# Group statistics of a convolution kernel: column sums on TensorE, and two loads per pair of channels

## The reference, cut to what matters

```python
def _gn(v, G=16, eps=1e-5):
    g = v.reshape(B_, G, C_ // G, H_, W_)
    m = jnp.mean(g, axis=(2, 3, 4), keepdims=True)
    s = jnp.var(g, axis=(2, 3, 4), keepdims=True)
    return ((g - m) / jnp.sqrt(s + eps)).reshape(v.shape)

x = x + _L0_conv_ref(_gn(x), weight, bias)          # 3x3 convolution, input and weights rounded to int8 levels
x = x + _L1_conv_ref(_gn(x), R_real, R_imag)        # low-frequency mixing of channels by rfft2 and irfft2
```

## Time and profile before

| | us |
|---|---|
| median of 3 runs | 3830.03 |
| range of the runs | 3829.28 to 3840.93 |
| the profiled execution | 3835.66 |
| its span, first to last instruction | 3833.7 |

### The profile page before, as it was taken

The page is one execution under the profiler, slowest core; times in us unless marked ns, Lnnn a source line. Parts: engine busy times, 40 slices in busy tenths (PEclk is TensorE's granted clock), DMA queues, the critical chain, the costliest instruction groups (busy, mean ns, idle before and its releaser), DMA issues.

```text
span 3833.7 us, 79482 instructions
## 1 busy us (share of the span) xinstructions
PE 2790.1 (73%) x31386; PEld 1545.5 (40%) x31481; DVE 3377.8 (88%) x3462; ACT 2547.4 (66%) x3507; POOL 823.1 (21%) x1040
## 2 busy tenths in 40 slices
PE   0010000069999999999999999898888888888886
PEld 0000000036666666666666666673222222222222
DVE  6999999999999999999999999559888888888887
ACT  8999999958888787878788888433333333333332
POOL 0000000035445454545454545200000000000000
PEclk9999999999999999999999999859999999999998
DMA  9999999989999999999999999629999999999998
GB/s 361 357 357 357 356 354 357 344 223 354 344 306 348 304 356 297 354 301 351 311 342 326 332 336 315 207 96 422 427 427 427 427 427 427 427 423 420 420 419 372
DMA packets 323941, 1352.20 MB, mean 353 GB/s; under 512 B 43600, under 2 KB 44848, under 8 KB 241616
## 3 DMA queue, kind: packets, MB, share of 16 engines
q1 hardware_dynamic: 204528, 811.10, 58.8%
q0 software_dynamic: 82272, 268.58, 19.6%
q10 hardware_dynamic: 36864, 268.45, 16.6%
HBM read 811.09 MB, written 536.87 MB: 352 GB/s over the span
## 4 chain that ended last, share of the span: by engine, by line
DMA 37%; DVE 32%; PE 13%; issue 11%; ACT 5%; SPq 0%; POOL 0%; ACTq 0%; DVEq 0%
DMA out<-ring 20%; DVE ring L568 11%; DMA ring<-in_x 9%; DMA ring<-x_scratch 7%; DVE area L550 6%; PE ps L713 4%; DVE area L545 4%; DVE area L554 3%; ACT area L300 3%; PE ps L724 2%; DVE ring L663 2%; DVE area L563 2%; ACT area L308 2%; PE ps L816 1%; PE ps L734 1%
## 5 line engine op out<-in xcount | busy, mean ns | idle before, releaser
L284 POOL DMA_DIRECT2D x_scratch<-ring x1024 | 817.1, 805 | 1613.6 <-DVE ring L568 1590.8
L858 PE MATMUL ps<-x,gj_s 128*128 128x512 bf16 x2977 | 772.1, 408 | 218.5 <-DVE ring L663 211.6
L713 PE MATMUL ps<-area,wq 128*32 128x512 bf16 x12264 | 766.0, 383 | 57.8 <-DVE ring L568 32.2
L663 DVE TENSOR_TENSOR ring<-ps,ring 128x1024 f32<-128x1024 f32 x512 | 603.3, 1220 | 162.6 <-DMA ring<-x_scratch 159.2
L568 DVE SCALAR_TENSOR_TENSOR ring<-ps,sc,ring 128x1024 f32<-128x1024 f32 x512 | 634.3, 1279 | 20.0 <-PE ps L713 12.9
L339 ACT ACTIVATE area<-ps 128x512 f32<-128x512 f32 x1024 | 552.9, 595 | 115.8 <-PE ps L724 115.1
L469 DVE TENSOR_REDUCE stat<-area 128x4096 f32 (+1 forms) x128 | 565.5, 4418 | 55.9 <-ACT area L308 55.9
L858 PEld LDWEIGHTS ps<-x,gj_s 128*128 128x128 bf16 x3072 | 296.0, 103 | 772.6 <-DVE ring L663 437.0
L686 PE MATMUL ps<-stat,mean_s 128*128 x256 | 74.5, 360 | 693.9 <-DVE area L463 652.8
L724 PE MATMUL ps<-id_s,ring 128*128 128x128 f32 x4096 | 561.4, 280 | 17.5 <-ACT area L339 16.7
L346 ACT ACTIVATE area<-ring,qtab 128x2048 bf16<-128x2048 f32 x256 | 513.1, 2004 | 0.0
(11 more groups left out here) (122 smaller groups left out, 2349.7 us busy)
## 6 DMA issues: line engine op xcount, KB each, us to landing
ring<-in_x SPq DMA_DIRECT2D x128, 2048.0 KB, 8.5
ring<-in_x SPq DMA_DIRECT2D x1024, 256.0 KB, 6.9
x_scratch<-ring POOLq DMA_DIRECT2D x1024, 256.0 KB, 6.6
ring<-x_scratch SPq DMA_DIRECT2D x256, 1024.0 KB, 10.0
out<-ring ACTq DMA_DIRECT2D x256, 1024.0 KB, 27.0
ring<-in_rt SPq DMA_DIRECT2D x1, 4096.0 KB, 13.7
area<-in_gj SPq DMA_DIRECT2D x1, 768.0 KB, 4.5
eh_s<-in_eh SPq DMA_DIRECT2D x1, 128.0 KB, 2.1
```

Of the source, the lines that this page charges most:

```text
L284: pool.dma_start(x1_rows[b, m, r], xslot(t % SL)[32 * r:32 * r + 32, :].rearrange("p (g w) -> p g w", g=4)).then_inc(s_x_out[t % SL], 16)
L663: nc.vector.tensor_tensor(half, ps[0][:, hj * 2 * HW:(hj + 1) * 2 * HW], half, ALU.add).then_inc(s_add, 1)
L713: last = mm(ps[0][32 * cg:32 * cg + 32, HW * g:HW * g + HW], wq[:, (3 * a + dw) * C:(3 * a + dw + 1) * C], src[:, 1 + dw:1 + dw + HW], sta ...
L858: last = mm(bank(j), gj_s[:, (j * 3 + v) * 128:(j * 3 + v + 1) * 128], (z12, z12, z13)[v][:, k % 2], start=(v == 0), stop=(v == 2))
```

## The change

Three things change in the first stage.

1. The sum of a group is taken on TensorE. The weight is `negm_s`, 128x32, filled with -1/N. Eight fp32 matmuls per group, each over 512 of the 4096 columns, write into one PSUM bank: the column slices j and j + 4 accumulate on partitions 32(j % 4) to 32(j % 4) + 31. What is left, 128x512 in PSUM, is summed over its row by ScalarE (even groups) or VectorE (odd groups) into a column of a new tile `part`. The mean matmul then multiplies this column by a matrix with ones in rows 0, 32, 64 and 96. The banks of the column sums are 0 to 3, those of the means 4 to 7.
2. TensorE's order becomes: column sums of group n + 1, then the mean of group n. The column sums wait for the landing of their group (both transfers, semaphore at 32 per use).
3. The two channels of a group are loaded by two transfers, each 128 partitions x 2048 numbers (8 KB), one behind the other on SP's queue. The first channel now fills the first half of every partition of the slot, the second the other half.

The loops of the first stage are also written out in full where they were loops of the program with four groups in their body. There is one more constant to load.

```diff
@@ -39,7 +39,7 @@
     x1 = nc.dram_tensor("x1_scratch", [B, C, HW, HW], F32, kind="Internal").ap()
-    x_groups = x.rearrange("b (g c) (p h) w -> (b g) (c p) (h w)", c=GC, p=64)
+    x_chan = x.rearrange("b c (p j) w -> (b c) p (j w)", j=NJ)
@@ -69,6 +69,8 @@
         bsel_s = sb("bsel_s", [NT, B])
+        negm_s = sb("negm_s", [128, C])
+        part = sb("part", [128, NT])
@@ -94,8 +96,7 @@
             return ps[k // 4][0:p, (k % 4) * 512:(k % 4 + 1) * 512]
-        junk_v = area[:, 0:FT // 2]
-        junk_a = area[:, FT // 2:FT // 2 + FT]
+        junk_a = area[:, 0:HW]
@@ -149,6 +150,7 @@
         s_g_in = [sem(f"group_landed{k}") for k in range(4)]
+        s_cols = sem("group_column_sums_done")
@@ -206,7 +208,7 @@
         s_add = sem("out_done")
-        NCONST = 12
+        NCONST = 13
@@ -215,17 +217,15 @@
                              (gsel_s[:], gsel), (bsel_s[:], bsel), (comb_s[:], comb),
-                             (gsum_s[:], gsum), (gbc_s[:], gbc), (pavg_s[:], pavg)):
+                             (gsum_s[:], gsum), (gbc_s[:], gbc), (pavg_s[:], pavg), (negm_s[:], negm)):
                 sp.dma_start(dst, src).then_inc(s_const, 16)
-            for k in range(4):
-                sp.dma_start(gslot(k), x_groups[k]).then_inc(s_g_in[k], 16)
-            with sp.Fori(1, NT // 4) as i:
-                for k in range(4):
-                    sp.wait_ge(s_sq, i * 4 + (k - 3))
-                    sp.dma_start(gslot(k), x_groups[ds(i * 4 + k, 1)].rearrange("o p f -> (o p) f")).then_inc(
-                        s_g_in[k], 16)
+            for n in range(NT):
+                if n >= 4:
+                    sp.wait_ge(s_sq, n - 3)
+                for c in range(GC):
+                    sp.dma_start(gslot(n % 4)[:, c * FC:(c + 1) * FC], x_chan[GC * n + c]).then_inc(s_g_in[n % 4], 16)
@@ -295,30 +295,24 @@
         def _(act):
-            def group_sum(k, landed, n):
-                act.wait_ge(s_g_in[k], landed)
-                act.activation(junk_a, gslot(k), ACT.Identity, accum_out=st(0, n)).then_inc(s_asum, 1)
-            def squares(k, n, free):
+            def group_sum(n):
+                act.wait_ge(s_cols, n + 1)
+                act.activation(junk_a, bank(n % 4), ACT.Identity, accum_out=part[:, n:n + 1]).then_inc(s_asum, 1)
+            def squares(n):
                 act.wait_ge(s_mean, n + 1)
-                act.activation(st(1, n), bank(k)[:, 0:1], ACT.Copy).then_inc(s_nmean, 1)
+                act.activation(st(1, n), bank(4 + n % 4)[:, 0:1], ACT.Copy).then_inc(s_nmean, 1)
                 act.wait_ge(s_nmean, n + 1)
-                if free:
+                if n >= 2:
                     act.wait_ge(s_max, n - 1)
-                act.activation(sqs[:, k % 2], gslot(k), ACT.Square, bias=st(1, n),
+                act.activation(sqs[:, n % 2], gslot(n % 4), ACT.Square, bias=st(1, n),
                                accum_out=st(2, n)).then_inc(s_sq, 1)
-            for k in range(4):
-                if k % 2 == 0:
-                    group_sum(k, 16, k)
-                if k:
-                    squares(k - 1, k - 1, k - 1 >= 2)
-            with act.Fori(1, NT // 4) as i:
-                for k in range(4):
-                    if k % 2 == 0:
-                        group_sum(k, i * 16 + 16, i * 4 + k)
-                    squares((k - 1) % 4, i * 4 + (k - 1), True)
-            squares(3, NT - 1, True)
+            group_sum(0)
+            for n in range(NT):
+                if n % 2 and n + 1 < NT:
+                    group_sum(n + 1)
+                squares(n)
@@ -458,27 +452,20 @@
             link(nc.vector.memset(ones_s[:], 1.0))
-            def group_sum(k, landed, n):
-                dve.wait_ge(s_g_in[k], landed)
-                nc.vector.scalar_tensor_tensor(out=junk_v, in0=gslot(k)[:, 0:FT // 2], scalar=0.0,
-                                               in1=gslot(k)[:, FT // 2:FT], op0=ALU.add, op1=ALU.add,
-                                               accum_out=st(0, n)).then_inc(s_dsum, 1)
-            def largest(k, n):
+            def group_sum(n):
+                dve.wait_ge(s_cols, n + 1)
+                nc.vector.tensor_reduce(part[:, n:n + 1], bank(n % 4), AXX, ALU.add).then_inc(s_dsum, 1)
+            def largest(n):
                 dve.wait_ge(s_sq, n + 1)
-                nc.vector.tensor_reduce(st(3, n), sqs[:, k % 2], AXX, ALU.max).then_inc(s_max, 1)
-            for k in range(4):
-                if k % 2:
-                    group_sum(k, 16, k)
-                if k:
-                    largest(k - 1, k - 1)
-            with dve.Fori(1, NT // 4) as i:
-                for k in range(4):
-                    if k % 2:
-                        group_sum(k, i * 16 + 16, i * 4 + k)
-                    largest((k - 1) % 4, i * 4 + (k - 1))
-            largest(3, NT - 1)
+                nc.vector.tensor_reduce(st(3, n), sqs[:, n % 2], AXX, ALU.max).then_inc(s_max, 1)
+            for n in range(NT):
+                if n % 2 == 0:
+                    group_sum(n + 1)
+                if n:
+                    largest(n - 1)
+            largest(NT - 1)
@@ -679,11 +666,24 @@
             pe.wait_ge(s_const, 16 * NCONST)
-            with pe.Fori(0, NT // 4) as i:
-                for k in range(4):
-                    pe.wait_ge(s_dsum if k % 2 else s_asum, i * 2 + (k // 2 + 1))
-                    mm(bank(k)[:, 0:1], mean_s[:], st(0, i * 4 + k), start=True, stop=True).then_inc(s_mean, 1)
+            def column_sums(n):
+                pe.wait_ge(s_g_in[n % 4], (n // 4 + 1) * 32)
+                if n >= 4:
+                    pe.wait_ge(s_mean, n - 3)
+                for j in range(8):
+                    g = j % 4
+                    last = mm(bank(n % 4)[32 * g:32 * g + 32, :], negm_s[:], gslot(n % 4)[:, j * HW:(j + 1) * HW],
+                              start=(j < 4), stop=(j >= 4))
+                last.then_inc(s_cols, 1)
+            column_sums(0)
+            for n in range(NT):
+                if n + 1 < NT:
+                    column_sums(n + 1)
+                pe.wait_ge(s_dsum if n % 2 else s_asum, n // 2 + 1)
+                if n >= 4:
+                    pe.wait_ge(s_nmean, n - 3)
+                mm(bank(4 + n % 4)[:, 0:1], mean_s[:], part[:, n:n + 1], start=True, stop=True).then_inc(s_mean, 1)
@@ -918,7 +918,7 @@
     return {n: np.ascontiguousarray(v, dtype=np.float32) for n, v in dict(
-        eh=eh, ew=ew, gj=gj, ei=ei, ident=np.eye(128), mean=np.full((128, 128), -1.0 / (GC * HW * HW)), gsel=gsel, bsel=bsel, comb=comb, gsum=gsum, gbc=gbc, pavg=pavg).items()}
+        eh=eh, ew=ew, gj=gj, ei=ei, ident=np.eye(128), mean=np.repeat(np.arange(128)[:, None] % C == 0, 128, 1), negm=np.full((128, C), -1.0 / (GC * HW * HW)), gsel=gsel, bsel=bsel, comb=comb, gsum=gsum, gbc=gbc, pavg=pavg).items()}
```

More of the change, by code:

```diff
@@ L24, with build @@
 NK = 2 * NS
-def build(nc, x, wt, bias, rt, eh, ew, gj, ei, ident, mean, gsel, bsel, comb, gsum, gbc, pavg, out):
+def build(nc, x, wt, bias, rt, eh, ew, gj, ei, ident, mean, gsel, bsel, comb, gsum, gbc, pavg, negm, out):
     B = x.shape[0]
```

## The result

The changed kernel took 3829.71 us (median of 20 runs, 3823.92 to 3836.87), the kernel before 3836.04 in the same comparison: ratio 0.9987, 95% interval [0.9981, 0.9993]. It is faster by 0.13% by the ratio (the medians lie 6 us apart), which is no change by the measure of the prediction; 82 us less than 3830.03 were forecast, and the range of 3696 to 3806 didn't hold it.

A forecast was written before the change was run, and what follows sets the result against it. ScalarE was taken to bound the first stage, then a three-group loop: (column sums + 5.0 + landing 7.7) / 3, mixed clock, 5.25 us per group; stage end 694.9, 82.0 us earlier, hence 3748 us; range 3696 to 3806.

The forecast's parts named there:

- The bound now: First stage before the change: ScalarE sets the pace at 5.86 us per group, then VectorE at 5.6, transfers only third.
- The column sums: Added on TensorE: eight fp32 matmuls per group, four side by side, 1.9 us at the upper clock, 3.6 at the lower.
- Rival (d): TensorE: column sums don't overlap four deep, 7.4 us per group, 192 us later, 4022; chance 0.12.
- The loop: First stage's new bound: column sums, 5.0 us of further work and issue to landing, spread over three groups; 5.25 us per group.
- The landing D: Time from a load's issue to its landing, in the first stage's loop: taken as 7.7 us.
- Rival (b): First stage: landings at their present median of 8.4 us, 5.67 us per group, 29 us earlier, 3801; chance 0.15.
- The share of the levels: TensorE's clock in the first stage: a third of the groups at the upper level, giving 5.25 us per group.
- Rival (c): First-stage transfers already at a limit of 357 GB/s for reads, 5.87 us per group, 3826, no change; chance 0.08.
- The split: Two loads per group: lands no later, at worst 0.13 us per group; 427 against 435 GB/s, inside the 4.9 us.

The follow-up runs named there:

- e4: Changed kernel with the mean of a group ahead of the next group's column sums on TensorE, short sum just ahead of its squares or largest; 3722.43 us, ratio 0.9715.
- e5: Changed kernel with its own order and split loads, but six slots for groups instead of four; 3727.28 us, ratio 0.9719.
- e11: Changed kernel with one more wait on SP: a group's loads are issued only once the group before has landed; 4044.8 us (one run).
- e1: Changed kernel with one transfer of 16 KB per partition per group instead of two, column sums on TensorE kept; 3839.04 us, ratio 1.0017.
- e3: Changed kernel with one transfer per group that still writes two pieces of 8 KB per partition; 3838.46 us, ratio 1.0012.
- e9: Changed kernel with TensorE's first stage as a loop of four groups instead of written out, same order and waits; 3835.56 us, ratio 1.0004.
- e7: Changed kernel with column sums that read one partition of the slot instead of 128; 3820.19 us, ratio 0.9958.
- e8: Changed kernel with eight more fp32 matmuls of 128 columns, result unused, behind each mean on TensorE; 3799.8 us, ratio 0.9914.
- e6: e4 with one transfer of 16 KB per partition per group instead of two; 3711.59 us, ratio 0.9676.
- e10: e6 with six slots for groups instead of four; 3712.12 us, ratio 0.9681.
- e2: Kernel before with only its first stage's loads split into two transfers of 8 KB per partition; 3838.0 us, ratio 1.0012.

## Why the prediction was wrong

**The bound now, right.** ScalarE set the stage at 5.88 us per group. The change took ScalarE and VectorE off the path as costed: the short sums took 0.590 and 0.690 us (0.6 and 0.7 forecast).

**The column sums, right.** 1.92 and 3.64 us at the two levels (1.9 and 3.6 forecast), four matmuls side by side; the mean is 387.4 / 128 = 3.03. Rival (d) didn't happen.

**The loop, right.** Landing n+1 to issue n+4 took 7.84 us; 3.0 + 5.0 = 8.0 was forecast. e4 and e5, which open the loop in two ways, gained 110 and 108 us on the kernel before. That "the mean matmul of group n stands in TensorE's order behind the column sums of group n+1" is shown to be what closes it over three groups.

**The landing D, wrong: the term that failed.** The passage is "here a load would be issued when the one before is nearly through, so I take 7.7". D was 9.58. A third of 1.9 us is 0.63 per group, times 126 it is 79 us, and that is nearly the whole gain that was forecast. Rival (b), late landings, had the right mechanism and too low an end: it took 8.4, the median of the earlier trace rows. The events of the kernel before show that this median lies between two kinds of landing, of which there are 58 each in groups 8 to 123. SP issued in pairs, some 4 and 7.7 us apart in turn. The first load of a pair was issued 1.5 us before the landing ahead of it and took 7.70; the second was issued 3.7 us before it and took 9.20. The forecast took the first kind for all. In the changed kernel the issue was 3.8 us before the landing ahead on average, the 48 loads issued over 4 us before it took 10.3, and the 32 issued only 2 to 3 us before it still took 8.85. So loads that bunch are a part of it and not all.

What the 1.9 us are. Against the kernel before, the middle engine is no later (7.68 and 7.75), and the last of the 16 engines is 1.90 us behind it where it had been 0.70. A group has landed only when all 16 are through. Against landings on empty engines (e11) the 2.1 us more are 0.6 of the middle engine and 1.5 of the last one. The split (e1, e3), the instruction fetches (e9) and, for the most part, TensorE's reads (e7) are not the cause. e11 shows what removes the spread: engines that are empty at each issue. The kernel before points the same way, with 0.41 us for the first load of a pair and 0.99 for the second.

How the spread builds up is open. In e7 it grows from 0.90 to 2.3 us over four loads behind one that was issued within 2.2 us of the landing ahead; but the same count in the changed kernel shows no growth (2.28 for that first load, 1.62 four loads later) and none in e9. So it is shown that the spread is there while loads are queued and gone when the engines are emptied, and not what delays an engine. In the changed kernel 93 of 100 packets of 8 KB took 0.3 to 0.4 us and single ones up to 2, and e11 has 94 of 100 like this with a spread of 0.37; in e4 all but 2 of 1000 took 0.3 to 0.4, and the spread was 1.60. The share of slow packets doesn't go with the spread. And no run has the loop of three groups at a small spread, so that the 79 us would come back is worked out, not measured.

**The share of the levels.** The mean of 3.03 us is what a third at the upper level gives ((1.92 + 2 x 3.64) / 3 = 3.07). By group it was 35 at the upper level throughout, 46 at the lower and 47 on both, so the weight was right, though it was guessed for landings 5.25 us apart and not 5.82, which makes it luck in part. e8 shows the price of it: 30 us between 3.0 and 2.1 us of column sums.

**Rival (c).** Reads alone go on at 421 to 428 GB/s in e4, e6 and e10. The rule of the Trainium skill ("DMA: Bandwidth & Descriptors", "Bandwidth") that the HBM share of 358 GB/s binds would have given the right time for the wrong reason; that of "HBM Reference" ("Specifications (TRN2)"), that a core alone goes well above its share, agrees with these rows. That both kernels stood at 357 to 361 GB/s was chance, and so was the unchanged time: one bound, ScalarE's 5.88 us per group, was taken away, and the next one, the loop's 5.82, happened to lie 0.06 below it.

**The split.** Forecast inside the 4.9, and it cost 0.07 us per group where the transfers bind (e6). Where the loop binds it cost nothing: e1 and e3, with one transfer, were if anything slower than the changed kernel (1.0017 and 1.0012 against 0.9987). Why isn't shown.

**The range.** It ended at T = 5.67. The row for its upper end was there: D had a maximum of 10.9, and a queued load took 9.36. With 9.4 the prediction's own sum gives (8.05 + 9.4) / 3 = 5.82 and 3820; with 10.9 it gives 6.3, more than ScalarE's time before. I had ruled out queueing on the ground that a load would be issued when the one before is nearly through. No row showed that, and the prediction's own 7.7 and 5.25 put each issue 2.45 us before the landing ahead of it.

## What to carry to other kernels

When an engine that paced a stage is relieved, write down the loop that then closes (landing, work, free slot, issue, landing), count over how many groups it spans, and cost its transfer by the queued landings of the trace, not by the best ones or by a median over both kinds. The gain was had by reordering: the mean ahead of the next group's sums, so that the loop spans four groups and not three, with one load per group, gives 3711.59 us, 3.2% below the kernel before (e6). Here the wait for a free slot said nothing by itself (429 us of 500 when the transfers starved, 419 when they were full); the DMA share (0.93 against 1.01) told the two apart.

## What the runs showed of the hardware

- The granted clock of the view reads 1.00 where TensorE was at the lower level and no change had yet been recorded. In e7 the first record stands at 798.8 us, and the view gives 1.00 from 100 to 600 us, while an instruction of 512 columns takes 1056 ns there (592 ns at the upper level in the changed kernel, 897 on average at a granted 0.71).
```profile
100.00:600.00 500.00, 358.68 (x1556) 93.33 (x1560) 403.06 (x130) 369.15 (x346) 0.00 (x0) 1.00 0.93 364
```
```profile
L675 PE MATMUL ps<-ring,negm_s 1*32 1x512 f32 x1920 | 436.4, 1056 | 203.7 <-DMA ring<-in_x 203.7
```
- Column sums that read one row ran at the lower clock for the whole stage (e7, TensorE 72% busy from 100 to 600 us); with all 128 rows it went up and down (changed kernel, 59% busy, 0.71 on average); with the additional matmuls of e8, 78% busy, it was at 0.96.
- Within a landing the last of the 16 transfer engines was 1.3 to 2.0 us behind the middle one in the kernels that took the column sums on TensorE and kept loads queued, 0.70 and 1.15 us in the kernel before and e2, and 0.37 us where the engines were emptied between loads (e11).
- Reads alone held 421 to 428 GB/s over 500 us (e4, e5, e6, e10).
